# A mixture-of-experts tower on one core: VectorE turns the last 64 columns of a tile's gated values in 32 by 32 blocks, and the place rows are spread from 128 partitions

## The reference, cut to what matters

```python
logits = x @ router_w.T                       # 448 tokens, 32 experts
probs = softmax(logits)
rw, sel = top_k(probs, 8)
rw = rw / sum(rw)
for e in range(32):                           # acc starts at zero
    w_e = sum(where(sel == e, rw, 0))
    h = silu(x @ wg[e]) * (x @ wu[e])         # 512 -> 192, twice
    acc = acc + (h @ wd[e]) * w_e             # 192 -> 512
```

## Time and profile before

| | us |
|---|---|
| median of 3 runs | 307.24 (306.87 to 307.67) |
| the profiled execution | 305.28 |
| its span, first to last instruction | 303.5 |
| TensorE busy | 284.3 (94%) |
| VectorE busy | 150.9 (50%) |
| ScalarE busy | 125.1 (41%) |
| GpSimd busy | 126.1 (42%) |

### The profile page before, as it was taken

The page is one execution under the profiler, slowest core; times in us unless marked ns, Lnnn a source line. Parts: engine busy times, 40 slices in busy tenths (PEclk is TensorE's granted clock), DMA queues, the critical chain, the costliest instruction groups (busy, mean ns, idle before and its releaser), DMA issues.

```text
span 303.5 us, 3905 instructions
## 1 busy us (share of the span) xinstructions
PE 284.3 (94%) x1159; PEld 145.9 (48%) x1159; DVE 150.9 (50%) x446; ACT 125.1 (41%) x213; POOL 126.1 (42%) x129
## 2 busy tenths in 40 slices
PE   4899999779999999999999999999999999998992
PEld 1345444445557355544545555465545455553231
DVE  2648999996988623243244322323332243313465
ACT  2348998999974321321321332132223213312101
POOL 3162212976520322164356336535633653455220
PEclk9999999999998599999999999999999999999998
DMA  7999999503998189699999999999999999996784
GB/s 244 344 417 425 381 405 337 173 0 134 322 324 281 42 285 313 204 270 322 316 304 349 306 312 341 337 323 312 349 324 319 313 350 304 296 298 89 139 236 133
DMA packets 27799, 85.53 MB, mean 282 GB/s; under 512 B 4209, under 2 KB 4337, under 8 KB 26785
## 3 DMA queue, kind: packets, MB, share of 16 engines
q1 hardware_dynamic: 19760, 64.78, 60.8%
q0 software_dynamic: 7488, 18.42, 26.0%
q10 hardware_dynamic: 530, 2.08, 2.5%
HBM read 72.34 MB, written 12.92 MB: 281 GB/s over the span
## 4 chain that ended last, share of the span: by engine, by line
PE 57%; DVE 17%; DMA 6%; issue 5%; ACT 3%; POOL 2%; POOLq 0%; DVEq 0%; ACTq 0%
PE ps L1161 25%; PE ps L1190 9%; PE ps L1182 6%; PE ps L1193 5%; DMA ring<-sum 3%; PE ps L1145 3%; DVE big L1441 2%; DVE stats L1325 2%; PE ps L1215 2%; PE ps L1048 2%; DMA sum<-w_t,add_idx 2%; PE ps L927 2%; DVE raw L1447 2%; DMA scrap<-token_rows,idx 1%; PE ps L1218 1%
## 5 line engine op out<-in xcount | busy, mean ns | idle before, releaser
L632 POOL DMA_INDIRECT scrap<-token_rows,idx x36 | 35.9, 998 | 92.2 <-DVE add_idx L1632 59.0
L646 POOL DMA_INDIRECT sum<-w_t,add_idx x32 | 51.3, 1604 | 18.6 <-issue 7.0
L864 ACT ACTIVATE w_t<-ps 128x512 f32<-128x512 f32 x36 | 21.4, 597 | 84.2 <-PE ps L1182 79.5
L1642 DVE COPY w_t<-ps 128x256 f32<-128x256 f32 x34 | 14.4, 424 | 62.0 <-PE ps L1218 50.6
L1637 DVE SCALAR_TENSOR_TENSOR w_t<-ps,scrap,w_t 128x192 f32<-128x192 f32 x32 | 13.2, 413 | 54.6 <-issue 44.5
L869 ACT ACTIVATE w_t<-ps 128x192 f32<-128x192 f32 x34 | 11.3, 331 | 55.9 <-PE ps L1161 46.8
L1161 PE MATMUL ps<-ring,w_t 128*128 128x384 f32 x96 | 33.1, 487 | 0.7 <-issue 0.7
L555 POOL TENSOR_TENSOR root_out<-root_in,minus_half 112x1 f32<-112x1 f32 x20 | 13.1, 657 | 45.7 <-DVE root_in L1342 45.6
L1161 PE MATMUL ps<-big,w_t 128*128 128x384 f32 x88 | 30.3, 487 | 0.0
L952 PE MATMUL ps<-raw,last 128*112 128x512 f32 x64 | 30.2, 624 | 0.0
L1182 PE MATMUL ps<-ident,scrap 128*128 128x128 f32 x144 | 24.9, 297 | 3.0 <-DVE h L1736 2.0
(11 more groups left out here) (213 smaller groups left out, 469.6 us busy)
## 6 DMA issues: line engine op xcount, KB each, us to landing
big<-in_ffn_gate_up SPq DMA_DIRECT2D x15, 768.0 KB
ring<-in_ffn_gate_up SPq DMA_DIRECT2D x13, 768.0 KB
raw<-in_ffn_gate_up SPq DMA_DIRECT2D x6, 768.0 KB
last<-in_ffn_gate_up SPq DMA_DIRECT2D x6, 768.0 KB
big<-in_ffn_w_down SPq DMA_DIRECT2D x15, 256.0 KB, 4.6
ring<-in_ffn_w_down SPq DMA_DIRECT2D x13, 256.0 KB, 4.7
big<-in_mlp_w_in SPq DMA_DIRECT2D x2, 1536.0 KB, 17.8
big<-in_mlp_w_in SPq DMA_DIRECT2D x2, 1280.0 KB, 20.4
```

The lines of the kernel that those rows point to most:

```text
L632: nc.gpsimd.indirect_dma_start(got[:, got_at(s), :], None, rows_dram[:, :], bass.IndirectOffsetOnAxis(ap=idx[:, s:s + 1], axis=0)).then_in ...
L646: nc.gpsimd.indirect_dma_start(acc_dram[m.two][:, :], bass.IndirectOffsetOnAxis(ap=add_idx[:, m.eight:m.eight + 1], axis=0), y[:, m.four, ...
L864: nc.scalar.activation(x_t[:, m.two, :, :], bank(2 + m.two).rearrange("p (c t) -> p c t", c=4), ACT.Copy).then_inc(xt_ready, 1)
L1642: nc.vector.tensor_copy(h_t[:, m.two, :, :], bank(6)[:, 0:2 * P].rearrange("p (c t) -> p c t", c=2)).then_inc(ht_ready, 1)
```

## The change

Three things change. First, in a tile (not in the lists) the second transpose of `hid`, line 1218, is gone; instead VectorE turns columns 128 to 191 by eight transposes of 32 by 32 (`turn_rest`) from `hid` straight to `h_t` in SBUF. `turn_rest(t)` stands behind `weigh(t)` and ahead of `find(t+4)`; it waits for `weigh` to have written, and for `y_done` of tile t-2, whose down products read the same part of `h_t`. The products of line 1193 wait for a new semaphore, `rest_ready`. Second, `turn_back` copies 128 columns instead of 256 in a tile. Third, `place` has 128 partitions instead of 32, those without an expert cleared to zero by GpSimd behind its last root; the copy that fills it waits for this clear; and the place rows of the tiles are products over 128 partitions. The lists' place rows keep 32.

```diff
-        place = after(TOK // 2).bitcast(F16)[0:NE, :]
+        place = after(TOK // 2).bitcast(F16)
...
             root(1 + NG)
+            nc.gpsimd.memset(place[:, :], 0.0).then_inc(consts, 1)
...
             act.wait_ge(rank_done, 1)
-            nc.scalar.activation(place[:, :], bank(0)[0:NE, 0:TOK], ACT.Copy).then_inc(place_ready, 1)
+            act.wait_ge(consts, 12)
+            nc.scalar.activation(place[0:NE, :], bank(0)[0:NE, 0:TOK], ACT.Copy).then_inc(place_ready, 1)
...
                 pe.wait_ge(idx_ready, m.upto(-1))
-                nc.tensor.matmul(bank(7)[:, 0:TOK], ident16[0:NE, m.t:m.t + 1].broadcast_to([NE, 128]), place[:, :],
+                nc.tensor.matmul(bank(7)[:, 0:TOK], ident16[:, m.t:m.t + 1].broadcast_to([128, 128]), place[:, :],
                                  start=True, stop=True).then_inc(place_done, 1)
...
                     rows_ = rest_rows(m.slot)
+                    pe.wait_ge(rest_ready, m.upto())
                     nc.tensor.matmul(bank(4 + m.two), h_t[rows_, m.two, 1, :], down_rest_of(m.slot), start=False, stop=True
...
-                nc.tensor.transpose(bank(6)[:, 0:P], hid[:, m.two, 0:P], ident[:, :])
-                if isinstance(m, Tile):
-                    a = P - IB * m.two
-                    last = nc.tensor.transpose(bank(6)[:, P:2 * P], hid[:, m.two, a:a + P], ident[:, :])
-                else:
+                last = nc.tensor.transpose(bank(6)[:, 0:P], hid[:, m.two, 0:P], ident[:, :])
+                if isinstance(m, Quad):
...
+            def turn_rest(m):
+                dve.wait_ge(hid_ready, m.upto())
+                wait(dve, y_done, m.upto(-2))
+                for a in range(0, P, 32):
+                    for b in range(0, IB, 32):
+                        last = nc.vector.transpose(h_t[m.two * IB + b:m.two * IB + b + 32, m.two, 1, a:a + 32],
+                                                   hid[a:a + 32, m.two, P + b:P + b + 32])
+                last.then_inc(rest_ready, 1)
+
             def turn_back(m):
                 dve.wait_ge(ht_done, m.upto())
+                if isinstance(m, Tile):
+                    nc.vector.tensor_copy(h_t[:, m.two, 0, :], bank(6)[:, 0:P]).then_inc(ht_ready, 1)
+                    return
...
                 weigh(m, got[:, got_at(m.eight), D + t:D + t + 1])
+                turn_rest(m)
                 if t + LEAD < NE:
                     find(Tile(t + LEAD))
```

More of the change, by code:

```diff
@@ L401, in program @@
         xt_ready = sem("xt_ready")
+        rest_ready = sem("rest_ready")
         silu_ready = sem("silu_ready")
@@ L1151, in place_lists @@
                 nc.tensor.matmul(bank(7)[:, TOK:TOK + NE], pick[:, m.i, :], ident_h[0:NE, 0:NE], start=True, stop=True)
-                nc.tensor.matmul(bank(7)[:, 0:TOK], pick[:, m.i, :], place[:, :], start=True, stop=True).then_inc(place_done, 1)
+                nc.tensor.matmul(bank(7)[:, 0:TOK], pick[:, m.i, :], place[0:NE, :], start=True, stop=True).then_inc(place_done, 1)
             def gate_up(m):
@@ L1250, in _ @@
             for t, b in ((0, 7), (1, 4), (2, 5), (3, 6)):
-                nc.tensor.matmul(bank(b)[:, 0:TOK], ident16[0:NE, t:t + 1].broadcast_to([NE, 128]), place[:, :],
+                nc.tensor.matmul(bank(b)[:, 0:TOK], ident16[:, t:t + 1].broadcast_to([128, 128]), place[:, :],
                                  start=True, stop=True).then_inc(place_done, 1)
```

## The result

The changed kernel takes 318.99 us (median of 4 runs, 318.44 to 319.55), the kernel before 307.46 beside it (4 runs). The ratio worked out from all runs is 1.0396, interval 1.0344 to 1.0448 (the quotient of the two medians alone is 1.0375): slower, and by 11.5 us where 6.4 were forecast. The profiled execution took 318.87 us (span 317.1, from the first to the last instruction). So the two traces differ by 13.6 us of span, and that is the number to be accounted for. (The traced execution of experiment 7 was a slow one, 320.57 us against a median of 316.14, so what is read from that trace is only indicative.)

A forecast was written before the change was run, and what follows sets the result against it. TensorE was taken to set the pace, with VectorE two thirds idle. Terms -3.2 (loop) + 7.3 (tables) + 0.8 (list counts) + 1.5 (tail) = +6.4 us on the median 307.24 gave 313.6 us, range 306.5 to 319.

The forecast's parts named there:

- pairs and both ends: Expert loop: 0.23 us saved per pair of tiles, 3.0 over 13 pairs, plus 0.2 at both ends: -3.2 us.
- the two tables: Tiles 4 and 8: TensorE waits for table results VectorE makes behind the blocks and find; 3.2 and 4.1 us lost, +7.3.
- list counts, `ht_ready`: `list_counts` ahead of `turn_back(3)`, for which `list_starts` waits: +0.6 us; the same wait at tile 8: +0.2.
- gathers in the loop: Later gathers in the loop cost nothing, each having about four tiles, two pairs, until its transposes.
- tail: After the loop: later last gather and scatters, 1.3 us, and 0.2 for the last `turn_back`: +1.5 us.
- the block: VectorE: each 32 by 32 transpose taken as 0.225 us, eight in 1.80 per tile, bounded by 0.10 and 0.25.
- the drain of the place row: TensorE: a 128-partition place row avoids waiting for an empty array, 0.49 down to 0.19 us, saving 0.30 each.
- the index wait: Even tile's place row waits for find behind the blocks; 0.30 and one 0.11 us vanish, 0.23 per pair kept.
- `rest_ready`, the clear and the shorter copy back: New wait before line 1193, clear of `place` on POOL and shorter `turn_back`: hidden, nothing charged; uncovered clear at most 0.56 us.
- The 0.01 per block: Sensitivity: each 0.01 us on a block shifts the total 1.3 us: 1.04 loop, 0.16 tables, 0.08 tail.
- Just enough; nothing is charged: Half pair with an odd tile: index ready 2.7 us after `y_done`, TensorE wants it about 2.9 after; no cost.
- the first rival: Cheap blocks on VectorE: 0.10 us each, eight in 0.80; 302.8 us, up to 306 if transfers can't follow; chance 0.14.

The follow-up runs named there:

- experiment 7: Changed kernel with only half of the gate and up weight columns loaded from tile 12 on: 316.14 us, ratio 1.0307.
- experiment 12: Changed kernel with each gather asked for five tiles ahead instead of four, blocks where they were: 314.81 us, ratio 1.0233.
- Experiment 3: Changed kernel with the blocks moved behind find and the tables at tiles 4 and 8 only: 311.07 us, ratio 1.0101.
- experiment 4: Changed kernel with blocks ordered to keep the partition group for four instructions in a row (some values wrong): 311.43 us, ratio 1.015.
- experiment 5: Kernel before with the wide (128-partition) place row alone, no blocks on VectorE: 305.24 us, ratio 0.9954.
- Experiments 1: Changed kernel with a tile's eight blocks moved behind its find and turn_back: 306.62 us, ratio 0.9972.
- experiment 8: Changed kernel with the blocks last in a tile and half of the gate and up columns loaded from tile 12 on: 299.58 us, ratio 0.9792.
- experiment 2: Changed kernel with two more buffers for the turned values, so blocks wait for y_done of four tiles ago: 309.67 us, ratio 1.0125.

## Why the prediction was wrong in size

The whole difference of 13.6 us of span, term by term. The loop's part is the start of the gate-up of tile 31: 270.31 before, 281.61 after, +11.3.

| term | forecast | measured | from |
|---|---|---|---|
| pairs and both ends | -3.2 | about -5.2 | 10.47 to 10.13, 13 times: -4.4; the tiles ahead of and behind them: -0.8, of which 0.4 ahead of tile 0 |
| the two tables | +7.3 | +7.1 | 3.06 and 4.00 |
| clock behind the holes | none | +3.2 | 1.13 + 3.79 and 4.44, against 0.66 + 2.75 and 2.75 |
| list counts, `ht_ready` | +0.8 | about +0.3 | what is left of 11.3 |
| gathers in the loop | 0 | +5.9 | the seven pairs over 10.13 that hold no table; experiment 12 has 5.7 |
| tail | +1.5 | +2.3 | 33.2 to 35.5 |

- **The step that failed** is in the tail's paragraph: "Inside the loop the later gathers cost nothing: each has about four tiles, two pairs, until its transposes". Two pairs would be 21 us. The trace of before had 10.0 from 197.92 to 207.93 (and 8.1 for the other tile of a pair). It was counted from the tile's number. But GpSimd asks for the rows of tile t + 4 only when the gate-up of t + 1 starts (197.92 and 197.94), and TensorE transposes them before the gate-up of t + 3, so less than two tiles of 5.2 us lie between. The changed kernel leaves 6.75 of the 10.0, and its trips take 7.3 to 7.9. The text had named the cover and what its loss would cost ("TensorE would stand in every pair"; from tile 12 to 24 it was every second one: the pair behind a wait has 8.06 us of cover, from 209.89 to 217.95). It hadn't read the cover, which was in the trace. Of the trip that trace showed only that 8.1 us were enough, and 4.3 for the last gather.
- **Missed: the clock.** The holes themselves were right to 0.1 us. That a hole of 3 to 4 us is followed by 3.4 us at 0.50 was in no row before, since TensorE had no such hole in that loop; the sum had no term for it. Experiment 3 shows it from the other side.
- **Right in kind, small in size: the tail.** The last gather was forecast to make 1.3. GpSimd issues it 0.85 us after the gate-up of tile 31, where before it was 0.1 ahead, and the transposes are 5.3 after that gate-up, not 4.2: 1.0. The other 1.3 is the read of the sums, 10.88 us for 9.53.
- **Right:** the block (0.216 us from eight in 1.73, forecast 0.225, bounds 0.10 and 0.25, and experiment 4 has 0.12 where nothing is held); the drain of the place row (0.30 each, 0.61 a pair in experiment 5); the index wait that swallows most of it; that `rest_ready`, the clear and the shorter copy back cost nothing. The 0.01 per block that the text weighed with 1.3 us also holds for the pairs: 0.1 less for the eight is the 10.13 in place of 10.24.
- **"Just enough; nothing is charged"** for the odd half pair was right: its place rows show no wait.
- **The transfers** stood in the forecast only under the first rival, as what may hold cheap blocks at 306. Experiments 1 and 8 bear it out in the time: 306.6 with full loads, 299.6 with half of them.

The range reached to 319, at whose edge the result is. That it comes so near is luck: the range was built from prices of blocks, and not from a gather that comes late or a clock that falls, which make 9.1 of the 13.6 us.

**Open.** How short a hole brings the drop of the clock is not settled: it came after 2.34 us in experiment 4 (passes of 4.44 for 2.75) and after 2.14 in experiment 2, and it didn't after the 2.05 ahead of 286.87 in the changed kernel, whose clock stayed at 1.00. Nor is it known why the move of one gather makes the kernel before slower by 0.6%. The 0.3 us for list counts is a remainder, not a reading. That the tail gives back most of any gain in the loop (the gate-up of tile 31 to the end of the span: 33.2 before, 39.2 with the blocks last, 39.1 with the place row alone, 38.0 in experiment 12) was shown. For experiments 1 and 5 the wait for the last gather and the clock behind it account for it; why that gather's trip is 7.0 to 7.2 us there, for 4.3 before, is open. It is 34.5 in experiment 8, with half of the loads.

## What to carry to other kernels

A free engine is not a free place in its queue: 1.7 us of work per tile on a VectorE that was one third busy made the kernel 12.4 us longer ahead of the search for an index than behind it (where the ratio was 0.9972), so ask first what is queued behind the new work and what the new work waits for. Measure the margin of every prefetch in the trace, from the instruction that asks to the one that uses, and subtract the trip under load; don't count it in iterations of the code. And price a hole on TensorE with the slow clock behind it.

## What the runs showed of the hardware

- Eight 32 by 32 transposes of float32 on VectorE take 1.70 to 1.73 us when each writes to another group of 32 partitions than the last, 0.98 when it stays for four in a row.
- After holes of 3.06 and 4.00 us TensorE's granted clock was 0.50 for 3.4 us each, and the passes in it took up to 847 ns for 486. Behind the second hole it was still 1.00 for the first 0.8 us of work (0.89 from 163 to 164).
- A gather of 128 rows took 7.3 to 7.9 us from GpSimd's instruction to its landing in the changed kernel's loop, which moves 303 GB/s from 170 to 250 us, and 4.4 at the loop's end (282.46).
- From 170 to 250 us the transfers moved 329 GB/s in the kernel before and in experiment 5, and 327 with the blocks last. There pairs were 10.2 us on average and TensorE was busy for 77.50 of the 80 us; with half the gate and up columns it was 79.63 of 80, at 295 GB/s.
- A busy share of the DMA engines above 1 was no measure of the bytes here: it was 1.03 at 295 GB/s and 1.06 at 329.
